# A post-norm layer on one core: five token dots leave VectorE, a Newton root moves ahead of a weight piece, and first-layer products stand ahead of the gate's

## The reference, cut to what matters

```python
qkv = x @ w_qkv.T                                     # x: 2 batches x 2048 tokens x 256
agent = q @ w_conv1                                   # one number per token
agent_attn = softmax((agent * scale) @ k, over 256 channels)
agent_v = softmax(v @ agent_attn, over 2048 tokens)   # logits: one dot of 256 per token
agent_v = agent_v @ v                                 # one row of 256 per batch
x = layernorm(x + softmax(agent[:, None], -1) * agent_v)
scores = softmax(x @ gate_w.T)                        # 8 experts
top_vals, top_idx = top_k(scores, 2)
z = sum over the two experts of weight * ((y * silu(g)) @ W2.T),  y, g = split(x @ W1.T)
z = z + shared gated MLP(x; Ws1, Ws2)                 # hidden width 384
x = layernorm(x + z)
```

## Time and profile before

| | us |
|---|---|
| median of 3 runs | 339.32 |
| lowest, highest run | 338.72, 341.7 |
| profiled execution, its own time | 339.15 |
| span of the profiled execution | 337.4 |
| PE busy in the span | 311.0 (92%) |
| DVE busy | 266.3 (79%) |
| ACT busy | 194.8 (58%) |
| POOL busy | 205.2 (61%) |

### The profile page before, as it was taken

How to read it: one execution, slowest core, us unless ns; L and a number is a source line. 1 busy time by engine, 2 the same in 40 slices (tenths; PEclk the granted TensorE clock), 3 DMA queues, 4 the chain that set the end, 5 groups by cost and what they waited for, 6 DMA issues and landing times.

```text
span 337.4 us, 7796 instructions
## 1 busy us (share of the span) xinstructions
PE 311.0 (92%) x2190; PEld 277.4 (82%) x2190; DVE 266.3 (79%) x1083; ACT 194.8 (58%) x442; POOL 205.2 (61%) x241
## 2 busy tenths in 40 slices
PE   3889799999999999999999999999999999999960
PEld 2456688769798879888889999999999999998850
DVE  2795679865888898885789877776799889998686
ACT  1045686637374646465445666666655588688473
POOL 5049650746768776875757544447576856868760
PEclk9979999899999999999999999999999999999996
DMA  7977420211192111153257544447988988876953
GB/s 227 374 257 258 149 65 0 85 48 65 67 254 70 65 65 67 66 159 119 97 159 249 153 152 131 139 140 166 241 234 218 226 208 198 234 219 182 354 198 124
DMA packets 31383, 54.63 MB, mean 162 GB/s; under 512 B 4880, under 2 KB 22544, under 8 KB 31344
## 3 DMA queue, kind: packets, MB, share of 16 engines
q1 hardware_dynamic: 23136, 29.82, 28.5%
q0 software_dynamic: 8208, 24.32, 25.6%
HBM read 29.73 MB, written 24.40 MB: 160 GB/s over the span
## 4 chain that ended last, share of the span: by engine, by line
PE 54%; DVE 17%; DMA 9%; POOL 8%; ACT 5%; issue 3%; SPq 2%; DVEq 0%; ACTq 0%
PE bank L1129 19%; PE bank L1163 10%; PE bank L1012 8%; POOL rows_in L596 4%; PE bank L1093 4%; DMA stage<-ws_t 4%; PE bank L1036 4%; PE bank L996 3%; DMA x<-rows_out 2%; POOL w1lo L552 2%; PE bank L1143 2%; DVE htlo L1468 2%; DVE xs L1259 2%; DVE mix L1462 2%; DMA rows_in<-x,slot 2%
## 5 line engine op out<-in xcount | busy, mean ns | idle before, releaser
L654 POOL DMA_INDIRECT rows_out<-stage,place x71 | 69.8, 983 | 49.0 <-ACT stage L831 32.5
L596 POOL DMA_INDIRECT rows_in<-x,slot x64 | 64.6, 1009 | 47.0 <-DVE slot L1374 30.5
L1129 PE MATMUL bank<-w1hi,bx 128*128 x284 | 64.0, 346 | 0.2 <-DVE bx L1483 0.2
L1129 PEld LDWEIGHTS bank<-w1hi,bx 128*128 128x128 f32 x284 | 48.3, 188 | 0.7 <-issue 0.7
L811 ACT ACTIVATE stage<-bank 128x384 f32<-128x384 f32 (+1 forms) x36 | 17.5, 487 | 36.6 <-PE bank L1129 36.5
L831 ACT ACTIVATE stage<-bank,weight 128x256 f32<-128x256 f32 x71 | 30.0, 470 | 11.0 <-PE bank L1163 9.5
L1129 PE MATMUL bank<-w1lo,bx 128*128 x142 | 36.3, 336 | 0.0
L1483 DVE TENSOR_TENSOR bx<-bank,bx 128x512 fp32r<-128x512 f32 (+1 forms) x36 | 24.5, 684 | 13.5 <-ACT bx L753 13.1
L1036 PE MATMUL bank<-ws2hi,hthi 128*128 128x256 f32 x96 | 28.7, 299 | 5.0 <-DVE htlo L1468 3.3
L1012 PE MATMUL bank<-xthi,ws1hi 128*128 128x512 f32 x96 | 31.6, 411 | 0.0
L1012 PE MATMUL bank<-xthi,ws1lo 128*128 128x512 f32 x96 | 30.5, 400 | 0.0
(11 more groups left out here) (251 smaller groups left out, 871.9 us busy)
## 6 DMA issues: line engine op xcount, KB each, us to landing
stage<-rows_in SPq DMA_DIRECT2D x71, 133.0 KB, 2.6
xs<-rows_out POOLq DMA_DIRECT2D x12, 512.0 KB, 6.1
xs<-x SPq DMA_DIRECT2D x8, 512.0 KB, 8.3
out<-xs SPq DMA_DIRECT2D x7, 512.0 KB
stage<-w_t SPq DMA_DIRECT2D x8, 384.0 KB, 3.9
rows_in<-clear SPq DMA_DIRECT2D x16, 133.0 KB
rows_out<-stage,place POOLq DMA_INDIRECT x71
stage<-w_t SPq DMA_DIRECT2D x2, 512.0 KB, 3.9
```

The lines of the kernel that those rows point to most:

```text
L596: pool.indirect_dma_start(rows_in[0:E * CAP, :], bass.IndirectOffsetOnAxis(slot[:, q * G + t, k:k + 1], 0), x2[q % 2][:, t, :], None).then ...
L654: pool.indirect_dma_start(rows_out[:, :], bass.IndirectOffsetOnAxis(place[:, 2 * j + b:2 * j + b + 1], 0), by[j % 4][:, b * C:(b + 1) * C] ...
L1129: mm = pe.matmul(bank_h[j % 2][:, b, 0:F], bx[j % 2][:, (2 * b + k) * P:(2 * b + k + 1) * P], w[:, bass.ds(e, 1), k, :], start=(a == 0), s ...
```

## The change

1. **Dots.** The last five token logits of batch 0 (`ALONE` = 11 to 15) leave VectorE. ScalarE copies the row they are multiplied with from PSUM to SBUF (`krow`); GpSimd multiplies it with five token tiles (`terms`, in tiles that are free then); ScalarE sums each with `accum_out`. VectorE does one more `agent` dot of batch 1 before its logits (`EARLY` 10 becomes 11) and starts them after the copy. `lane_max(0)` also waits for the sums.
2. **Weight pieces.** Pieces 0 and 1 change places: the shared second layer's weights (768 columns) come first. `high` and `low` stand elsewhere in ScalarE's and GpSimd's order: `value_exp(0)` before `high(1)`, `high(4)` after the first `rows_hi`, `high(5)` inside group 0, `high(6)` to `high(9)` at the heads of groups 1 to 4.
3. **Root.** `rough_rstd(0)` moves ahead of `low(3)`, and `rough_rstd(1)` stays ahead of `low(5)` but behind `low(4)`. Tile 3's variance is taken on VectorE (`first_variance`, three instructions) and no longer by a square on ScalarE.
4. **TensorE.** Forty `warm` products around the first transposes are gone. The transposes go in the order 0, 2, 3, 1. In group 0 the first half of `first_layer(0, 0)` stands ahead of the gate's products, starts on `xthi` alone, and multiplies with `xtlo` last.
5. **VectorE.** `channel_max(1)` and `channel_sum(1)` come later; some semaphores are merged.

```diff
-        EARLY = 10
+        EARLY = 11
+        ALONE = TB - 5
         DOTS = ([("agent", 0, t) for t in range(TB)] + [("agent", 1, t) for t in range(EARLY)]
-                + [("logit", 0, t) for t in range(TB)] + [("agent", 1, t) for t in range(EARLY, TB)]
+                + [("logit", 0, t) for t in range(ALONE)] + [("agent", 1, t) for t in range(EARLY, TB)]
...
+        krow = sums1[:]
+        terms = [x2[1][:, 0, 0:C], x2[1][:, 2, 0:C], x2[1][:, 3, 0:C], x2[0][:, 3, 0:C], row0[:]]
...
                 tiles = slice(g * G, (g + 1) * G)
-                pool.wait_ge(s_sq, (g + 1) * G)
+                pool.wait_ge(s_sq, squared((g + 1) * G))
+                if g == 0:
+                    pool.wait_ge(s_first_var, 3)
...
             token_shift(0)
             token_softmax(0)
-            low(0)
+            pool.wait_ge(s_dotsum, 1)
+            for n, t in enumerate(range(ALONE, TB)):
+                pool.wait_ge(s_x[t // G], 16)
+                pool.tensor_tensor(terms[n], xs[:, t, :], krow, ALU.mult).then_inc(s_term, 1)
             pool.wait_ge(s_ghi, 1)
             pool.tensor_tensor(gate[:, :, 1, :], gatef[:], gate[:, :, 0, :].bitcast(F32), ALU.subtract).then_inc(s_glo, 1)
+            low(0)
+            token_shift(1)
             low(1)
             low(2)
-            token_shift(1)
+            rough_rstd(0)
             low(3)
-            low(4)
-            rough_rstd(0)
             pool.wait_ge(s_first[1], 2)
             token_softmax(1)
+            low(4)
+            rough_rstd(1)
             low(5)
-            rough_rstd(1)
...
             channel_exp(0)
-            high(0)
+            act.wait_ge(s_pe[0], pe_at("r"))
+            act.activation(krow, token_bank[0][:, 0:C], ACT.Copy).then_inc(s_dotsum, 1)
+            for n, t in enumerate(range(ALONE, TB)):
+                act.wait_ge(s_term, n + 1)
+                act.activation(terms[n], terms[n], ACT.Identity, accum_out=lv[:, 0, t:t + 1]).then_inc(s_dotsum, 1)
             act.wait_ge(s_gate, 16)
             act.activation(gate[:, :, 0, :], gatef[:], ACT.Copy).then_inc(s_ghi, 1)
+            high(0)
+            value_exp(0)
             high(1)
             high(2)
-            value_exp(0)
+            token_exp(1)
             high(3)
-            token_exp(1)
-            high(4)
             statistics(0, 2)
             channel_exp(1)
-            high(5)
...
             rows_hi(0)
-            high(6)
+            high(4)
             statistics(1)
-            high(7)
             act.preload_act_table(ACT.Silu)
             for g in range(LAST):
-                if 2 <= g <= 3:
-                    high(6 + g)
+                if 1 <= g <= 4:
+                    high(5 + g)
...
                 silu(g, 2)
+                if g == 0:
+                    high(5)
                 hidden_hi(g, 2)
...
             token_column(1)
-            warm(20, banks[1])
...
-                for t in range(G):
+                for t in (0, 2, 3, 1):
...
-                    steps = [(w, xt, k) for w, xt in ((ws1hi, xthi), (ws1hi, xtlo), (ws1lo, xthi)) for k in range(KC)]
+                    terms = ((ws1hi, xthi), (ws1hi, xtlo), (ws1lo, xthi))
+                    if g == m == h == 0:
+                        pe.wait_ge(s_xhi, KC)
+                        terms = ((ws1hi, xthi), (ws1lo, xthi), (ws1hi, xtlo))
+                    steps = [(w, xt, k) for w, xt in terms for k in range(KC)]
...
             def group(g):
+                if g == 0:
+                    first_layer(g, 0, [0])
                 logits_of(g)
-                first_layer(g, 0)
+                first_layer(g, 0, [1] if g == 0 else (0, 1))
...
             first_transposes()
-            warm(8, banks[4])
             token_row(1)
-            warm(12, banks[4])
...
+            def first_variance():
+
+                vec.wait_ge(s_add, G)
+                vec.bn_stats(bst[:, 0, :], xs[:, G - 1, :]).then_inc(s_first_var, 1)
+                vec.wait_ge(s_first_var, 1)
+                vec.bn_aggr(mv[:, G - 1, :], bst[:, 0, :]).then_inc(s_first_var, 1)
+                vec.wait_ge(s_first_var, 2)
+                vec.tensor_scalar(square[:, G - 1:G], mv[:, G - 1, 1:2], float(C), None, ALU.mult).then_inc(s_first_var, 1)
...
-            agents(1, range(7, EARLY))
-            token_logits(0, range(TB))
+            agents(1, range(7, EARLY - 1))
+            vec.wait_ge(s_pe[0], pe_at("r"))
+            agents(1, range(EARLY - 1, EARLY))
+            vec.wait_ge(s_dotsum, 1)
+            token_logits(0, range(ALONE))
...
             layer_norm(0, range(G))
+            first_variance()
             sums_spread(1)
+            layer_norm(1, range(0, 2))
             channel_max(1)
-            layer_norm(1, range(0, 2))
-            channel_sum(1)
             inverse_std(0)
```

55 lines of the change are left out of this document (34 added, 21 removed).

## The result

The changed kernel takes 343.48 us (median of 19 runs, 342.22 to 348.07) against 340.41 of the kernel before on the same chip (19 runs, 337.73 to 344.56): ratio 1.0113, 95% interval 1.0078 to 1.0148. The ratio compares the means of each kernel's fast runs; the two medians are 0.9% apart. It is slower by about one per cent. The profiled execution took 344.06 us (span 342.3), 4.9 us of span more than the one of the kernel before.

The account below looks back on a forecast made before the run. The prediction took serial front work, then from 46 us mostly TensorE's chain, as the bound. Terms +2.3 - 0.3 - 0.7 + 2.6 = +3.9, clock +0.4, on 339.15 gave 343.5 us; range 337.0 to 346.0.

Parts of the forecast that it names:

- Part 1: Five dots moved off VectorE: lane maximum 0.7 us earlier, hidden by TensorE's unread products; +0.1 us to the exponentials.
- Part 2: First root ahead of a GpSimd weight piece: root starts at 36.85 instead of 37.98, -1.1 us.
- Part 3: `low(3)` directly behind the root holds up VectorE's refinement by 3.4 us; the last scale comes +2.3 with the earlier root.
- Part 4: TensorE's transposes -0.3, first products and ScalarE's queue before the first silu -0.7, clock fall while TensorE idles +0.4 us.
- Part 5: `low(5)` in group 0 holds up VectorE's `sel` and `htlo`, delaying TensorE's third chunk: +2.6 us, next gate at 65.5.
- Rival C: Longer clock fall: TensorE idles before the third chunk, half clock in groups 0 and 1; 345.5 to 346 us, 8 in 100.
- Rival A: No holding up: GpSimd's long piece lets VectorE's refinement through; 337.0 us, 22 in 100.
- rival B: Only the first collision: `low(5)` misses `sel` and `htlo` in group 0; 340.2 us, 14 in 100.

Follow-up runs that it names:

- e4: Kernel before with only the first root moved between `low(3)` and `low(4)`, so `low(4)` follows the root; 359.07 us, ratio 1.0123.
- f4: f3 with `low(3)` also moved behind the second batch's token softmax; 341.34 us, ratio 1.0017 to the kernel before.
- f2: The changed kernel, unaltered, run again beside the kernel before on another occasion; 345.68 us, ratio 1.0131.
- f3: Changed kernel with `high(4)` and `high(5)` one place earlier on ScalarE and `low(5)` behind the second refinement; 343.49 us, ratio 1.0080.
- e1: Changed kernel with `low(3)` moved from directly behind the first root to behind the second token softmax; 356.60 us, ratio 1.0063.
- e6: Changed kernel with the 40 unread `warm` products put back around the first transposes; 360.62 us, ratio 1.0211.
- e2: Changed kernel with `low(5)` cut into six instructions of 256 columns; 358.47 us, ratio 1.0102.
- e3: e1 with `low(5)` also moved out of the front, cut into 256-column parts, and later pieces one group later; 359.80 us, ratio 1.0160.
- e5: e1 with VectorE doing all 16 dots again, the row copy kept; 357.31 us, ratio 1.0121 to the kernel before.
- e7: Kernel before with the change's order of TensorE's first work and of ScalarE's last four pieces, unread products kept; 354.26 us, ratio 1.0020.
- f1: The kernel before, unaltered, run for a trace on the chip of f2, f3 and f4; one time, 340.38 us.
- e8: e7 with the first root behind `low(3)`, and `low(4)` and `low(5)` behind the second token softmax; 353.56 us, ratio 0.9998.

## Why the prediction was right

The forecast was 343.5 us with the larger part of its chance on "slower"; the median is 343.48. That the two agree to a hundredth is luck. The forecast was 4.3 us on top of a first trace of 339.15; the kernel before has a median of 340.41 over 19 runs, and the medians are 3.1 us apart, the means behind the ratio 3.8. So the base was low and the difference high, and within the difference several terms were off and cancelled. What was right is the mechanism that carries it: two collisions, at the places and with nearly the lengths foretold. e4 puts one into the kernel before and gets the loss; f4 takes both out of the change and the loss goes.

- **Part 1 (the dots), forecast +0.1.** The lane maximum came at 25.78, not 25.2, but the load had landed 1.25 late: behind the first dot it is 17.58 against 18.94 before. The forecast held that TensorE's row of 54 unread products hides it. This rests on TensorE's clock, which fell to half before that row's execution (they took 3.48). In `after` and in f2 the clock did not fall, the row ended at 25.70, and the maximum was waited for (0.30 ahead of 26.00): 1.56 gained from the first dot to the transposition. In the executions of f3, f4, e1 and e6 it fell, the row ended behind the maximum, and the distance is 19.08 to 19.71, as in the kernels without the dots (19.05 to 19.88; e2 and e3, where the clock fell earlier still, have over 20). So where the clock falls between 20 and 24 us the dots bring nothing that stands out of this scatter (0.5 between e5 and e1), and 1.56 is dots and full clock together: no trace without the dots has the full clock there. The term was right for the first kind of execution and wrong in the profiled one.
- **Part 2 (the root), forecast -1.1.** From the transposition to `vareps` it is 10.44 us now, and was 11.67 before: -1.23. The working named a wrong reason on the way: I had `first_variance`'s last instruction held up until the piece ended. It ran at 35.71 in 0.15, inside the piece of 32.85. The root waited for the piece on its own engine, which ends at the same time, so the number stood.
- **Part 3 (the piece behind the root), forecast 3.4.** Measured 3.46 for 0.16, so 3.3; `rn` took 3.38 in f2, 3.41 in f3, 3.39 to 3.49 in e2, e4, e6. With part 2, +2.3 was forecast; from the transposition to `minus` +2.06 came. The earlier trace rows had shown the hold-up only with pieces of 0.71, and the step from there to 3.5 was the risky one; it held. The Trainium skill says in SBUF — State Buffer, "SBUF: two separate sides", that the lock is held for the whole instruction; for pieces of GpSimd that stream, these rows agree.
- **Part 4 (transposes, products, silu), forecast -0.6 from `minus` to the silu** (-0.3, -0.7, +0.4 for the clock). Measured -0.19. The granted clock was indeed 0.76 from 40 to 44 us. Where it did not fall (e1, e3, e5: 1.00 throughout) the same work takes 8.00, so the fall cost 0.8 here, twice the term. What is left, -1.0, is the forecast's -0.3 and -0.7, but not for its reasons: e7 has the reordering and a ScalarE queue shorter still, keeps the unread products, and gets 0.26. Most of the gain goes with the unread products, whose removal the forecast had put at nothing; e6 gets 1.6 longer with them back. TensorE idled 3.61, where the forecast had some 3.
- **Part 5 (the last piece), forecast +2.6, gate of group 1 at 65.5.** `sel` took 3.00 and the gate came at 66.11. From the silu to it the forecast's own figures give 14.7 for the 12.51 before; it is 15.45. Mechanism and victim as forecast, the size 0.7 short; in f2 it is 15.39. The piece started 0.4 later than foretold, and the third chunk ran at the lower clock.
- **What was mis-sized: the clock behind it.** Rival C had the second fall of the clock at 8 in 100. It happened: from the gate of group 1 to that of group 2 it is 22.04 for 20.50, and the same +1.6 in f2. TensorE is busy through the whole of it in both kernels, but works at the lower clock from the gate at 66.11 to about 72.8, some 6.7 us, against 3.4 before; half of the difference is 1.65 (an estimate from the granted clock), about the 1.54 lost. The idle time ahead of it is TensorE's wait for the third chunk (1.72 busy of 4.00). f3 and f4, without `sel` held, have 20.57 and 20.68. That a fall always follows isn't shown: e6 has `sel` held too (3.00), and its clock stays at 1.00 from 47 to 77 us. The Trainium skill (TensorE: Matmul & The Clock Gate, "Part 1: The HAM clock gate") says that the point of change varies from run to run, and I had expected the change to scatter by it. The runs don't tell: the twelve runs of f2 span 5.7 us and those of f4 2.3, but the nineteen of the kernel before span 6.8 in the first comparison. In the profiled execution the 1.56 of the first column made up for what this fall cost.
- Rival A (no holding up) and rival B (only the first collision) fell with the two VectorE rows. The groups behind gave back 0.6 and the tail 0.5 in this execution; the last column of f1 and f2, 226.13 and 225.59, differs by as much.

## What to carry to other kernels

An instruction moved on one engine has to be laid beside the other engine's instructions at its new time: here GpSimd's long streaming pieces cost nothing beside VectorE's reads of PSUM, and nearly their whole length ahead of five instructions of 0.16. A duration of twenty times the usual in a timeline, ending with a neighbour's, points to a hold-up, and the lists of waits don't show it. When such a collision is removed, look for the next victim of the same piece, and for the queue behind which the piece now stands; in e1, e2, e3, f3 and f4 that is where time went. A gain has to be taken apart in the same way: with the unread products left in, the new order of TensorE's work brought 0.26 us (e7), and most of what it seemed to bring went with those products.

## What the runs showed of the hardware

- The hold-up depends on VectorE's operands. Beside GpSimd pieces of 1536 columns, these ran at their usual durations: token dots with one operand in PSUM, BN_STATS (0.43 at 35.03 in after), BN_AGGR (0.18), a [128, 1] `tensor_scalar` (0.15), MAX8 (0.38) and FIND_INDEX8 (0.16) of the route beside the piece of 47.12 (end 50.64). Held to the piece's end were `tensor_tensor` with both operands in SBUF, of 4, 32 and 512 columns. A [128, 4] `tensor_scalar` was held too (1.15 in e1, 1.19 in e3, and 0.67 beside parts of 256 columns). Why four columns are held and one is not, these runs don't settle.
- A held instruction ends 0.02 (`rn` of 37.78 in after) to 0.55 us (`htlo` of 52.93 in f4) behind GpSimd's piece; the second is most of its own 0.68. So it looks stopped before it begins, rather than slowed.
- Not every GpSimd instruction holds VectorE. `htlo`, 512 columns from SBUF, keeps its 0.69 inside GpSimd's [128, 4] power of 1.04 (69.96 in 69.77 before; 70.88 in 70.61 in f1; 74.62 in 74.36 in e4).
- GpSimd isn't slowed in turn by an instruction that it holds: the pieces that hold VectorE take 3.48 and 3.49, as others do (3.50). Six parts of 256 columns take 5.04 in e2, with VectorE's instructions in between.
- The same kernel before took 339 to 341 us (medians) in the first and the last comparison and 353 to 354 in the two between, on other chips. Up to group 1's gate the distances of f1 and e7 agree within 0.8 us; from group 2's gate to the last block product it is 226 us in the kernel before and 238 to 240 in the kernels e (but e3). There TensorE idles 3.3 us before and 10.7 to 12.2 in e1, e2, e4, e5 and e7, part of it put down to "issue", and the pages of e1, e3, e4 and e8 have waits of ScalarE for "remote". The kernel before has no trace on these chips, and what the waits are was not looked into.
